# Rounding the square sums for the matmul, summing the value squares first, and moving two splits and a layer norm to other units

## The reference, cut to what matters

```
x = x + LN(attention(LN(x)))
x = x + LN(ffn(LN(x)))

attention: xq = rms_norm(x @ wq.T) * q_norm_w     # 2048 features, 32 heads of 64
           xk = rms_norm(x @ wk.T) * k_norm_w     # 512 features, 8 heads
           xv = x @ wv.T
           scores = xq xk / 8 + ALiBi bias, window of 256 tokens back; softmax; times xv; @ wo.T
ffn:       silu(x @ gate.T * gate_s) * (x @ up.T * up_s) @ down.T * down_s    # 1408 inner features
```

## Time and profile before

| | |
|---|---|
| median of 3 runs | 1191.52 us (1191.12 to 1192.47) |
| the profiled execution, its own time | 1192.52 us |
| its span, first to last instruction | 1190.7 us |
| granted TensorE clock | 0.998 of full speed |
| PE, DVE, ACT, POOL busy | 97%, 75%, 62%, 26% of the span |
| stage 1 / stage 2 / the rest, from the chain | to about 293 us / to about 884 us / to the end |

### The profile page before, as it was taken

One profiled execution on the slowest core, in us unless ns is written; L12 is line 12 of the kernel. 1 busy time (PEld: TensorE's weight loads), 2 busy tenths in 40 slices (PEclk: granted clock), 3 DMA queues, 4 the chain that ended last, 5 costly groups with the idle time before them and its releaser, 6 DMA issues.

```text
span 1190.7 us, 26659 instructions
## 1 busy us (share of the span) xinstructions
PE 1156.7 (97%) x9016; PEld 988.1 (83%) x9016; DVE 890.4 (75%) x2329; ACT 743.8 (62%) x1583; POOL 304.8 (26%) x354
## 2 busy tenths in 40 slices
PE   6999999999899999999999999999999999999997
PEld 5878888887777889898988998898988888888876
DVE  5587878687899888888888888888866575645464
ACT  4655556455899888888888888888853443222230
POOL 3000000000588843324242323233211100202022
PEclk9999999999999999999999999999999999999999
DMA  5316355346667775556655674557435540303020
GB/s 177 106 45 230 160 194 218 119 193 239 201 240 240 250 223 184 170 186 208 205 177 183 205 216 150 165 167 225 139 118 202 168 140 2 107 1 107 1 71 37
DMA packets 100898, 189.55 MB, mean 159 GB/s; under 512 B 9376, under 2 KB 39072, under 8 KB 100768
## 3 DMA queue, kind: packets, MB, share of 16 engines
q1 hardware_dynamic: 100768, 187.88, 47.1%
HBM read 116.22 MB, written 71.63 MB: 158 GB/s over the span
## 4 chain that ended last, share of the span: by engine, by line
PE 90%; DVE 4%; issue 2%; ACT 2%; DMA 0%; POOL 0%; SPq 0%; DVEq 0%; POOLq 0%; ACTq 0%
PE bank L1419 22%; PE bank L1553 19%; PE bank L1484 14%; PE bank L1357 12%; PE bank L1445 11%; PE bank L1463 3%; PE bank L1461 3%; PE bank L1462 3%; PE bank L1473 2%; DVE stats L1021 1%; DVE pT_lo L1181 1%; DVE pT_lo L1177 1%; ACT p_sb L806 1%; DVE u_sb L1058 1%; PE bank L1530 1%
## 5 line engine op out<-in xcount | busy, mean ns | idle before, releaser
L806 ACT ACTIVATE p_sb<-u_sb,low 128x384 f32<-128x384 f32 (+2 forms) x512 | 271.8, 535 | 61.9 <-DVE low L1058 57.7
L1058 DVE CUSTOM_DVE_ANT_0 u_sb<-bank,bias 128x384 f32<-128x384 f32 (+2 forms) x512 | 229.4, 452 | 46.8 <-PE bank L1357 24.4
L1357 PE MATMUL bank<-k_st,q_st 128*128 128x384 f32 (+2 forms) x1024 | 251.7, 328 | 3.1 <-DVE low L1058 3.1
L1445 PE MATMUL bank<-ident,p_sb 128*128 128x128 f32 x1152 | 217.4, 279 | 14.5 <-DVE pT_lo L1177 5.2
L1177 DVE TENSOR_TENSOR pT_lo<-bank,pT_hi 128x384 f16<-128x384 f32 (+2 forms) x394 | 179.0, 454 | 26.9 <-ACT pT_hi L917 18.6
L1357 PEld LDWEIGHTS bank<-k_st,q_st 128*128 128x128 f32 x1024 | 168.6, 191 | 20.0 <-DVE low L1058 3.7
L1445 PEld LDWEIGHTS bank<-ident,p_sb 128*128 128x128 f32 x1152 | 140.7, 141 | 45.7 <-ACT p_sb L806 18.2
L917 ACT ACTIVATE pT_hi<-bank 128x384 f16<-128x384 f32 (+2 forms) x394 | 159.7, 405 | 28.7 <-PE bank L1445 25.1
L699 POOL TENSOR_TENSOR o_out<-o_raw,inv_sum 128x256 f32<-128x256 f32 x128 | 79.9, 626 | 320.8 <-DVE inv_sum L1189 320.8
L1553 PE MATMUL bank<-zT_hi,gu 128*128 128x512 f32 x352 | 139.2, 395 | 0.6 <-DVE hid L1308 0.6
L1553 PE MATMUL bank<-zT_lo,gu 128*128 128x512 f32 x352 | 138.1, 392 | 0.0
(11 more groups left out here) (135 smaller groups left out, 2302.2 us busy)
## 6 DMA issues: line engine op xcount, KB each, us to landing
q_st<-q_scr SPq DMA_DIRECT2D x32, 1024.0 KB, 8.1
q_scr<-qk SPq DMA_DIRECT2D x61, 512.0 KB, 2.7
k_st<-k_scr SPq DMA_DIRECT2D x64, 256.0 KB, 3.3
o_scr<-o_out SPq DMA_DIRECT2D x128, 128.0 KB, 3.8
o_in<-o_scr SPq DMA_DIRECT2D x16, 768.0 KB, 5.2
z_in<-z_scr SPq DMA_DIRECT2D x8, 1024.0 KB, 6.2
k_scr<-qk SPq DMA_DIRECT2D x12, 512.0 KB, 2.7
v_scr<-v_out SPq DMA_DIRECT2D x4, 1040.0 KB, 6.4
```

What stands on the lines that cost most here:

```text
L806: nc.scalar.activation(p_sb[:, u % RING, 0:w], u_sb[:, u % RING, 0:w], ACT.Exp, scale=-1.0, bias=low[:, u % RING:u % RING + 1]).then_inc(p ...
L1058: nc.vector.tensor_tensor_reduce(out=u_sb[:, u % RING, 0:w], in0=bank[u % 2][:, 0:w], in1=bias[2 * u // UNITS][:, u % REP, at:at + w], sca ...
L1357: mm = nc.tensor.matmul(bank[u % 2][:, 0:w], q_st[:, s, r, P * i:P * i + P], k_st[:, s, part, P * key:P * key + w], start=(part == 0), sto ...
L1445: mm = nc.tensor.transpose(bank[probability_bank(A)][:, P * j:P * j + P], p_sb[:, u % RING, P * j:P * j + P], ident[:])
```

## The change

1. **Sums in two rounded parts.** ACT rounds each sum of squares to `sum_hi` (`round_sum`, after the square of unit 16 and after the first value copy, unit 20), DVE makes `sum_lo` (`split_sum`, first thing at units 17 and 21), and PE multiplies both with a rounded matrix of ones: two fp32r matmuls in place of one float32 matmul. The sums move to after units 18 and 21 in all batches, the roots and inverses to units 19 and 22. `sum_lo` lies where the first `square` buffer lies.
2. **Value squares summed once.** `square_v` moves from unit 15 to 13; DVE adds the four squares at unit 14 (`sum_v`, three additions); PE makes one float32 matmul with ones in place of four.
3. **Split at unit 4.** The left-over query block is rounded at the end of unit 2 and split at the end of unit 4.
4. **Projected tile.** Statistics at unit 13, normalisation at 15; POOL makes the inverse root just before it adds the residual, after the second block of heads has been finished.

```diff
+SQUARE_V_AT = QC - 3
+SUMS_AT = (QC + 2, QC + KVC + 1)
-ROOT_AT, LATE_INVERSE_AT = (QC + 2, QC + KVC + 1), 4
+ROOT_AT, LATE_INVERSE_AT = (QC + 3, QC + KVC + 2), 4
-TAKE_Y_AT, STATS_AT, NORM_AT = 0, 2, 6
+TAKE_Y_AT, STATS_AT, NORM_AT, LAST_STATS_AT = 0, 13, 15, 2
-LAST_EARLY_AT = 5
+LAST_EARLY_AT = (2, 4)
@@ POOL, attend(n)
-                        if i == TT // 2 and tile > 0:
-                            inverse_root(1, y_var, tile, y_rstd)
-                    if i == 0 and tile > 0:
+                    if i == 1 and tile > 0:
+                        inverse_root(1, y_var, tile, y_rstd)
                         add_residual(tile - 1)
@@ ACT
+            def round_sum(b, n):
+                act.wait_ge(acc_ready, NSQ * b + (NSQ if n else QC - 1))
+                at_least(act, ssq_psum, 2 * b + n)
+                nc.scalar.activation(sum_hi[:], sum_sq[:, n], ACT.Copy).then_inc(sum_hi_ready, 1)
-                        if first and n == QC - 1:
+                        if first and n == SQUARE_V_AT:
                             square_v()
+                            if n in (1, SUMS_AT[0]):
+                                at_least(act, ssq_psum, 2 * b + n // QC)
                         nc.scalar.activation(dst, bank[n % 4][:], ACT.Square).then_inc(sq_ready, 1)
+                        if n == QC:
+                            round_sum(b, 0)
+                        if n == QC + KVC:
+                            round_sum(b, 1)
@@ DVE
+            def sum_v():
+                for k, (to, other) in enumerate(((2, 3), (0, 1), (2, 0))):
+                    dve.wait_ge(v_squared, KC)
+                    if k == 2:
+                        dve.wait_ge(v_summed, 2)
+                    to, other = raw[QC + to], raw[QC + other]
+                    nc.vector.tensor_tensor(to, to, other, ALU.add).then_inc(v_summed, 1)
+            def split_sum(b, n):
+                dve.wait_ge(sum_hi_ready, 2 * b + n + 1)
+                nc.vector.tensor_tensor(sum_lo[:], sum_sq[:, n], sum_hi[:].bitcast(F32), ALU.subtract).then_inc(sum_ready, 1)
+                        if n == QC + 1:
+                            split_sum(b, 0)
+                        if first and n == SQUARE_V_AT + 1:
+                            sum_v()
                         if first and n == QC + 1:
                             scale_v()
+                        if n == QC + KVC + 1:
+                            split_sum(b, 1)
@@ PE
-                nc.tensor.matmul(bank[6 + n][:], ones[:], sum_sq[:, n], start=True, stop=True).then_inc(ssq_psum, 1)
+                nc.tensor.matmul(bank[6 + n][:], ones_r[:], sum_hi[:], start=True, stop=False)
+                nc.tensor.matmul(bank[6 + n][:], ones_r[:], sum_lo[:], start=False, stop=True).then_inc(ssq_psum, 1)
-                        for kc in range(KC):
-                            pe.wait_ge(v_squared, kc + 1)
-                            mm = nc.tensor.matmul(bank[7][:], ones[:], raw[QC + kc], start=(kc == 0), stop=(kc == KC - 1))
-                        mm.then_inc(v_norm_psum, 1)
+                        pe.wait_ge(v_summed, KC - 1)
+                        nc.tensor.matmul(bank[7][:], ones[:], raw[QC + 2], start=True, stop=True).then_inc(v_norm_psum, 1)
-                    if n == QC + 1:
-                        sum_squares(b, 0)
-                    if n == QC + KVC + first:
-                        sum_squares(b, 1)
+                    if n in SUMS_AT:
+                        sum_squares(b, SUMS_AT.index(n))
```

More of the change, by code:

```diff
@@ L260, in sandwich_layer @@
             raw_first = sb(s1, "raw_first", [P, LATE_OWN, T])
-            square = sb(s1, "square", [P, 2, T])
+            with ExitStack() as before_sums:
+                square = sb(before_sums, "square", [P, 2, T])
+            sum_lo = sb(s1, "sum_lo", [P, T], F32R)
+            sb(s1, "second_square", [P, T])
             sum_sq = sb(s1, "sum_sq", [P, 2, T])
@@ L270, in sandwich_layer @@
             raw_last = sb(s1, "raw_last", [P, QC + KVC - LATE_OWN, T])
+            sb(s1, "bias_room", [P, REP * WIN + 16])
+            sum_hi = sb(s1, "sum_hi", [P, T], F32R)
+            ones_r = sb(s1, "ones_r", [P, P], F32R)
             raw = [raw_first[:, f] if f < LATE_OWN else raw_last[:, f - LATE_OWN] for f in range(QC + KVC)]
@@ L350, in sandwich_layer @@
         held = sem("held")
+        ones_r_ready, sum_hi_ready, sum_ready = sems("ones_r_ready sum_hi_ready sum_ready")
+        v_summed = sem("v_summed")
         ident_ready = sem("ident_ready")
@@ L667, in _ @@
                                         op=ALU.pow).then_inc(tile_rstd[i], 1)
+            nc.gpsimd.tensor_copy(ones_r[:], ones[:]).then_inc(ones_r_ready, 1)
             pool.wait_ge(gemm_done, 1)
@@ L952, in _ @@
                     unit_work(n, u)
-                    if n == 0 and u == LAST_EARLY_AT:
+                    if n == 0 and u == LAST_EARLY_AT[0]:
                         round_raw(B - 1, LATE - 1)
@@ L1233, in _ @@
                         split_v(B - 1, NGEMM - 1)
-                    if n == 0 and u == LAST_EARLY_AT:
+                    if n == 0 and u == LAST_EARLY_AT[1]:
                         split_raw(B - 1, LATE - 1)
@@ L1249, in _ @@
                 unit_work(B * TT - 1, u)
-                if u == UNITS + STATS_AT:
+                if u == UNITS + LAST_STATS_AT:
                     stats_y(B * TT - LAG - 1, bank[7])
@@ L1377, in sum_squares @@
             def sum_squares(b, n):
-                pe.wait_ge(acc_ready, NSQ * b + (NSQ if n else QC - 1))
-                pe.wait_ge(sq_ready, (QC + KVC) * b + (QC + KVC if n else QC))
+                if n == 0 and isinstance(b, int) and b == 0:
+                    pe.wait_ge(ones_r_ready, 1)
+                pe.wait_ge(sum_ready, 2 * b + n + 1)
                 at_least(pe, root_ready, 2 * (b - 1) + n + 1)
```

## The result

The changed kernel took 1201.24 us (median of 4 runs, 1200.34 to 1202.12), the kernel before 1191.78 beside it: a ratio of 1.0083, 95% interval 1.0067 to 1.0099. It is slower by 9.5 us, within the range of 1190 to 1202, though near its upper end, and 2.8 above the 1198.4 forecast; the likeliest case's own band, 1195.5 to 1201, is missed by 0.2. The profiled execution took 1200.71 us with a span of 1198.9, against 1190.7 before: 8.2 us of span to explain.

The account below looks back on a forecast made before the run. The prediction took PE, busy 97% of the span, as the bound. Its terms, 5.55 - 1.1 + 1.05 - 1.85 + 3.2 = +6.85 us on a median of 1191.5, gave 1198.4 us, range 1190 to 1202.

Parts of the forecast that it names:

- Batch 0, value squares: Before unit 16: PE waits from 59.3 to 62.4 for DVE's additions; the 2.6 us saving gone and some 0.5 more.
- Batch 0, value weights: Batch 0: split_sum ahead of scale_v, and block 5's split_weights after unit 18's addition, start unit 20 at 80.1; batch +5.55 us.
- Batches 1 and 2: Rounded sums save 0.80 us in each batch, 0.24 given back by a wait at unit 21; -1.1 us together.
- rival (d): Sums on PE: rounded ones do not speed the matmul, two passes at 0.43 us; kernel 1200 us; chance 0.04.
- Batch 3: Batch 3 into the attention: last inverse one unit later, first bias addition at 293.9 instead of 292.84; +1.05 us.
- Step 0: Split at unit 4 escapes POOL's bias, but the scaling at unit 8 is held; 1.85 us saved, between 0.9 and 2.8.
- One of the forecast's signs: Step 0, unit 8: the scaling, held by POOL's bias, would take near 1.7 us in the profile after.
- Steps 5 to 15: Tile's move: 0.46 us gained per tile, 0.76 lost from units 13 to 15 on; net +0.30, eleven tiles +3.2 us.
- (a): Batch 0: value weights arrive in time for unit 20, giving its full 3.4 us; kernel 1189.5 us; chance 0.09.
- (b): Steps 5 to 15: DVE's slack at units 13 to 15 swallows the statistics; -5.1 for +3.2, 1190.1 us; chance 0.12.
- (c): Attention pays the full 0.76 without gain, the stall at units 3 and 4 having another source; +8.4, 1203.6 us; chance 0.05.
- (e): Unit 17, six steps: POOL's residual addition meets DVE's scaling, up to 0.5 us each; 1201.4 us; chance 0.05.

Follow-up runs that it names:

- experiment 1: Changed kernel with scale_v put ahead of split_sum on DVE at unit 17 of batch 0; 1194.79 us, 1.0024 of the kernel before.
- (2): As experiment 1, with split_weights of block 5 also back from the inverse to unit 18; 1193.41 us, ratio 1.0013 to the kernel before.
- experiment 4: Changed kernel plus 36 matmuls nobody reads in PE's two long waits of batch 0; 1197.13 us, ratio 1.0044 to the kernel before.
- experiment 6: Kernel before with only the early split (left-over block rounded at unit 2, split at unit 4 of step 0); 1189.72 us, ratio 0.9978.
- experiment 5: Changed kernel with the projected tile's move undone (statistics at unit 2, normalisation at 6); 1200.16 us, ratio 1.0071 to the kernel before.
- experiment 7: Kernel before with only the projected tile moved (statistics at unit 13, normalisation at 15); 1194.22 us, ratio 1.0019.
- experiment 9: Kernel before with the early split, and the tile's statistics at unit 27, normalisation at 29; 1184.21 us, ratio 0.993.
- 3: As (2), with PE's value norm moved behind unit 16, before unit 17; 1192.93 us, ratio 1.0011 to the kernel before.
- 8: Changed kernel, tile undone, order of (2), scale_v at unit 16, value squares summed by PE in four unrounded parts ahead of unit 15; 1191.13 us, ratio 0.9997.
- 10: Changed kernel with only the value part undone (squares at unit 15, four unrounded parts ahead of unit 16); 1198.22 us, ratio 1.0054 to the kernel before.

## Why the prediction was right, and where it was off

**Batch 0, value squares: right.** The additions came at 59.94 and were 0.70 apart, the last ending at 62.0 (forecast 62.3), and PE was released at 62.08 (62.4).

**Batch 0, value weights: the mechanism right, the term too small.** Both moves named in the forecast do what it says. Putting them back gave 6.4 us (experiment 1) and 1.4 more (2). Unit 20 began at 81.47, not at 80.1, and batch 0 ended 9.01 us later, not 5.55. But for the scatter named above, the missing 3.46 is one omission: every matmul was priced at 0.227 us, also right behind a wait of 3 and one of 5 us. They ran 0.43 apart, and the filled waits of experiment 4 put this at 3.57 us. The first part of it made unit 16 end late, so the whole chain behind it (reciprocal at 69.84 for 68.4) was late by 1.4; the second came at units 20 and 21. The forecast wrote down both waits and never asked what the clock does behind them.

**Batches 1 and 2: right**, -0.92 for -1.1. PE's sum matmuls are 0.23 apart, which ends rival (d).

**Batch 3: right.** From its start to the first bias addition 68.10 us (233.86 to 301.96) for 67.07 before: +1.03, forecast +1.05.

**Step 0: right in kind, at the far end of its bounds.** From that addition to step 1 it is 30.17 us (332.13 - 301.96) for 32.70: -2.53 where 1.85 was taken out of 0.9 to 2.8. One of the forecast's signs failed: in the changed kernel the scaling at unit 8 was not held (1.7 us forecast). It began as POOL's bias ended:

```profile
306.19 2.75 POOL L700 TENSOR_TENSOR bias<-dist,slopes 128x1536 f32<-128x1536 f32 x1 [100.24 <-DVE low L1080]
...
308.91 0.74 DVE L1133 SCALAR_TENSOR_TENSOR raw_first<-raw_first,norm_w,inv_rms 128x512 f32<-128x512 f32 x1
```

That start is 6.95 us behind the first bias addition, for 6.15 in experiment 6, and in between DVE waited for PE's scores (0.74 and 0.38 us), with PE's clock at 0.57 from 304 to 308 us. In experiment 6 the scaling was held, for 1.39 us, and the clock stayed up. Every trace with the early split is one of these two kinds, and the stretch to step 1 takes 30.0 us in the kind with the held scaling and 30.2 to 30.4 in the other. So the deduction made for the scaling, about 1 us, is the term that was too large. The forecast also left out that the old split's wait of 2.83 us had the lower clock behind it; how much of the gain that is was not tested.

**Steps 5 to 15: gain right, cost nearly, net too high.** The gain at unit 4 is 0.49 (forecast 0.46). The cost is 0.04 + 0.38 + 0.27 = 0.69 at units 15 to 17 (0.76). 0.1 comes back at units 19 to 26, which the forecast had denied. A difference of two near numbers, 0.09 a tile instead of 0.30, is then 1.15 us in the trace against 3.2 (0.30 eleven times is 3.3, which the forecast had as 3.2). The part cost 1.1 us in the changed kernel (experiment 5) and 2.2 alone (experiment 7), where units 15 and 17 are 0.04 and 0.03 longer and units 19 to 26 give less back. The other traces put both inside one scatter: from step 5 to the last scores, the seven kernels with the tile at units 13 and 15 take 423.94 to 425.13 us and the four with it at 2 and 6 take 422.54 to 422.89. On average that is 1.7 us, and at the most 2.6.

**The rivals.** (a), the value weights in time, is out: unit 20 waited 5.3. (b), the slack of units 13 to 15, is out, and experiment 9 shows where such slack is. (c) is out, since the gain came. (e): in step 6 the residual addition (521.14 to 522.42) and the scaling at 522.32 (0.75 us) hardly met.

**The sum.** +8.20 for +6.85 in the spans: 3.46 too little in batch 0 and 0.55 in the last stage, which the change does not touch (311.76 to 312.57 us in the experiments' traces, so scatter), against 2.05 too much in the steps and 0.70 in batch 3 and step 0. The nearness of the total owes something to errors of opposite sign.

## What to carry to other kernels

An engine that follows its list in order passes on every wait: before a new instruction goes in, ask what it waits for and what is queued behind it. Here a 0.69 us split, which waited for another unit's sum, held a chain of 10 us. Price a new wait on TensorE with its clock behind it: two waits of 3.2 and 5.3 us cost another 3.6 us in slow matmuls. Take that price as a range, for behind nearly equal waits it was 1.6 us in the changed kernel and 2.9 in experiments 1 and 2 (from the value norm to unit 17: 5.31, 6.60 and 6.64 us, against 3.71 with the wait filled). And put movable work where the engine's next product has the most time in hand, read unit by unit: units 13 to 15 gave back all of the gain at unit 4, units 27 to 29 none of it, and only the second is faster (by 8.2 us with the early split, of which the split alone is 2.3).

## What the runs showed of the hardware

TensorE's clock fell to its lower level after waits of 3.2 and 5.3 us (the changed kernel) and of 2.83 us (step 0 of the kernel before). Over waits of 1.1 and 1.8 us it stayed at the upper one in batch 0 (experiments 3 and 8). The longest wait alone does not decide it: in step 0 every kernel with the rounded sums has the same wait of 1.4 us, and behind it the clock fell in the changed kernel and in experiments 4, 5 and 8 and stayed up in experiments 1, 2, 3 and 10. In batch 0, 36 matmuls whose result nobody read kept it up and made the kernel 4.1 us faster. A DVE instruction with two SBUF inputs was held by POOL's bias in a new place once the old one was freed (0.74 to 1.39 us, experiment 6), so such a conflict can move with the work; in the changed kernel it did not.
